# Attention memory: normalisation, query taps and the decay product put on other engines, retrieval and output products in array tiles

## The chip, the cores and the metric

The kernel runs on one core of one Trainium2 chip. The time is the device time in microseconds of one execution. The kernel before was run three times: 972.88 us is the median, 970.96 and 977.67 are the ends. The profile is that of one execution, whose span from the first to the last instruction is 973.9 us.

## The reference

The program is a block of three residual layers on x of 8 x 1024 tokens with 256 features: a mixture of experts (half weight), the attention with a memory, and the mixture of experts again. Only the attention is touched. For each batch element and chunk of 128 tokens it computes

```python
k, v, q = conv(hidden @ Wk.T), conv(hidden @ Wv.T), conv(hidden @ Wq.T)   # causal, 4 taps, per channel
alpha = (sigmoid(hidden @ aW.T + ab) * 0.1).mean(-1)                      # eta, theta alike
for c0 in range(0, S, CHUNK):
    g = grad(W_state, k[:, sl], v[:, sl]) * GRAD_SCALE                    # per token, clipped in norm
    # per token: S = eta * S - theta * g;  W = (1 - alpha) * W + S
    h = silu(einsum('btd,btod->bto', q[:, sl], W1t))
    outs.append(einsum('bto,btpo->btp', h, W2t))
out = concatenate(outs) @ Wo.T
out = out * rsqrt(mean(out * out) + EPS) * norm_g
return out * (hidden @ gW.T + gb)
```

where hidden is the layer norm of x. The kernel does not make the state of each token. It writes the retrieval as a product with the state at the chunk's start, scaled by a decay (AB), plus products of scores and gradients, weighted by scans over the tokens (M).

## The kernel before, in words

The attention takes the eight chunks (NCH = 8) of all eight batch elements at a time; most tiles are 128x1024, that is eight blocks of 128x128. Features or tokens lie on the partitions. Each engine has its own program, written out in `step(c, ...)`, and a queue runs it strictly in order; semaphores join them. `step(c)` mixes three chunks: it ends chunk c-1 (second half of its output), computes chunk c (gradients, new state, second hidden layer, retrieval, first half of the output) and prepares chunk c+1 (projections, convolution, rates, scans, gates, keys). VectorE also takes the moments of chunk c+2 (L974 to L988) and normalises it (L990). Steps 0 to 5 have this part (`norm_too`), steps 6 and 7 do not; step 7 prepares nothing.

What matters around the change:

- VectorE: after the gradients (L1141) it runs `stats_of(c+2)`, `moments_of(c+2)`, the split of the sigmoids (L1003), `convolve(c+1)` with taps on key/value and query in turn (L1012, L1019), `second_hidden(c)` (L1152, makes hid2), the last query tap (L1029), `decayed_hidden` (L1156, hid2 times AB), the momentum scans (L1034), the score product P2 (L1160), the carry and memory scans, the gate additions for pairs 0 and 1, the decay scans, `split_retrieved` (L1007), the other gate additions, and `normalise(c+2)` (L990).
- GpSimd: `gradient_norm` (power), `norm(c+2)` (power, waits for var_done), then `prep(c+1)`, and the powers and additions of the output.
- ScalarE: it copies from PSUM, makes the first query tap with the bias (L1297), the sigmoids, the copies of the new state (L1363), the second sigmoid (`second_hidden`, L1355), the rates keep and eta (L1309), the retrieved block (L1359).
- TensorE: `new_state`, `second_hidden`, `turn_state` (waits for state_copied), `rates`, `gram`, `second_scores`, `gates` 0 and 1, `retrieve`, `gates` 2 and 3 (wait for gate_read), `outputs(c, 0)`, `keys`, `hidden`, then the next step with `turn_x(c+2)` as its first part.

PSUM is cut in four pairs of banks A, BB, C, DD. `retrieve` writes 64 partitions of all of DD, one batch element after the other. `outputs` multiplies by Wo in three passes of high and low halves (`passes`, L1466), with 64 rows of the array each.

## Time and profile before

| | us |
|---|---|
| median of three runs | 972.88 |
| lowest and highest | 970.96, 977.67 |
| span of the profiled execution | 973.9 |
| TensorE busy | 794.4 (82%) |
| VectorE busy | 700.0 (72%) |
| ScalarE busy | 420.9 (43%) |
| GpSimd busy | 245.6 (25%) |

The attention takes about 255 to 766 us of the span, the first mixture of experts lies before it and the second behind it. A row of a timeline reads: start in us, duration in us, engine, line, operation, output and inputs, forms, count; at its end in brackets the time that the engine stood idle before it and what ended that. Lines are those of the kernel before.

### The profile page before, as it was taken

How to read it: one execution, taken by the hardware profiler on the slowest of the kernel's cores; microseconds unless marked ns; L12 is line 12 of the kernel's file. 1: busy time of each engine (PE TensorE's matmuls, PEld its weight loads, DVE VectorE, ACT ScalarE, POOL GpSimd, SP SyncE). 2: the span in 40 equal slices, each digit the busy share in tenths (PEclk: the TensorE clock that was granted, in tenths of full speed). 3: DMA queues.
4: the chain of work that ended last, by engine and by line, in shares of the span. 5: the costliest groups of instructions: out<-in, count | busy, mean ns of one | idle time of the engine just before them, and what ended most of it. 6: DMA issues, size and time to landing. Idle time of an engine off the chain costs nothing. (4 is left out here: it accounts for less than half of the span.)

```text
span 973.9 us, 15603 instructions
## 1 busy us (share of the span) xinstructions
PE 794.4 (82%) x5632; PEld 722.8 (74%) x5632; DVE 700.0 (72%) x1644; ACT 420.9 (43%) x837; POOL 245.6 (25%) x172
## 2 busy tenths in 40 slices
PE   5921989999266899999999999999877423999996
PEld 1311889999255788989888898989867412999996
DVE  0085759774558899999999998998832185877861
ACT  1202626542042738274573738365432103654650
POOL 0005432131101214060332414050321105423112
PEclk9955799999678999999999999999958555999999
DMA  5886842400310103012120303002020144545100
GB/s 186 301 302 181 256 162 99 152 27 15 100 43 1 44 2 115 16 60 71 44 86 0 129 0 96 33 0 86 1 87 1 50 166 146 184 128 176 54 23 28
DMA packets 58018, 88.91 MB, mean 91 GB/s; under 512 B 6705, under 2 KB 48881, under 8 KB 57841
## 3 DMA queue, kind: packets, MB, share of 16 engines
q1 hardware_dynamic: 46848, 70.44, 22.1%
q0 software_dynamic: 3840, 10.49, 3.3%
q10 hardware_dynamic: 7280, 7.34, 2.4%
q8 instruction: 28, 0.46, 0.2%
q14 instruction: 22, 0.17, 0.1%
HBM read 74.63 MB, written 22.02 MB: 99 GB/s over the span
## 5 line engine op out<-in xcount | busy, mean ns | idle before, releaser
L519 PE MATMUL ps<-weights_high_down,moe_hidden_high 128*128 128x256 f32 (+1 forms) x384 | 109.0, 284 | 2.6 <-DVE moe_rows L394 2.6
L521 PE MATMUL ps<-weights_high_down,moe_hidden_low 128*128 128x256 f32 (+1 forms) x384 | 107.9, 281 | 0.0
L520 PE MATMUL ps<-weights_low_down,moe_hidden_high 128*128 128x256 f32 (+1 forms) x384 | 107.9, 281 | 0.0
L519 PE MATMUL ps<-moe_normedT_high,weights_high_up 128*128 128x320 f32 x256 | 82.7, 323 | 2.1 <-DVE moe_hidden_low L386 1.0
L520 PE MATMUL ps<-moe_normedT_low,weights_high_up 128*128 128x320 f32 x256 | 80.7, 315 | 0.0
L521 PE MATMUL ps<-moe_normedT_high,weights_low_up 128*128 128x320 f32 x256 | 80.6, 315 | 0.0
L386 DVE SCALAR_TENSOR_TENSOR moe_hidden_low<-ps,moe_hidden_high 128x320 fp32r<-128x320 f32 x128 | 62.6, 489 | 21.1 <-ACT moe_hidden_high L481 18.3
L481 ACT ACTIVATE moe_hidden_high<-ps 128x320 fp32r<-128x320 f32 x128 | 56.2, 439 | 38.3 <-PE ps L521 25.5
L461 ACT CAST weights_high_up<-weights_raw_up 128x256 fp32r<-128x256 f32 x128 | 43.8, 404 | 64.1 <-PEq L104 64.1
L519 PEld LDWEIGHTS ps<-weights_high_down,moe_hidden_high 128*128 128x128 f32 (+1 forms) x384 | 69.3, 181 | 2.8 <-issue 2.8
L521 PEld LDWEIGHTS ps<-weights_high_down,moe_hidden_low 128*128 128x128 f32 (+1 forms) x384 | 69.4, 181 | 0.0
L520 PEld LDWEIGHTS ps<-weights_low_down,moe_hidden_high 128*128 128x128 f32 (+1 forms) x384 | 69.4, 181 | 0.0
L889 POOL TENSOR_TENSOR att_QAB<-att_Q,att_AB 128x1024 f32<-128x1024 f32 x8 | 19.0, 2376 | 195.9 <-DVE att_AB L1064 195.9
L461 ACT CAST weights_high_down<-weights_raw_down 128x256 fp32r<-128x256 f32 x128 | 45.9, 402 | 31.5 <-PE ps L521 31.5
L519 PEld LDWEIGHTS ps<-moe_normedT_high,weights_high_up 128*128 128x128 f32 x256 | 49.8, 194 | 4.7 <-issue 2.9
L1467 PE MATMUL ps<-att_w_high,att_xT_high 128*128 128x320 f32 x128 | 43.5, 340 | 11.4 <-DVE att_theta_pre L1081 11.4
L394 DVE SCALAR_TENSOR_TENSOR moe_rows<-ps,moe_prob,moe_rows 128x256 f32<-128x256 f32 (+3 forms) x48 | 23.1, 482 | 40.2 <-PE ps L521 39.5
L380 DVE TENSOR_TENSOR weights_low_down<-weights_raw_down,weights_high_down 128x256 fp32r<-128x256 f32 x128 | 49.2, 416 | 2.0 <-ACT weights_high_down L461 1.4
L520 PEld LDWEIGHTS ps<-moe_normedT_low,weights_high_up 128*128 128x128 f32 x256 | 49.7, 194 | 0.0
L521 PEld LDWEIGHTS ps<-moe_normedT_high,weights_low_up 128*128 128x128 f32 x256 | 49.6, 194 | 0.0
L380 DVE TENSOR_TENSOR weights_low_up<-weights_raw_up,weights_high_up 128x256 fp32r<-128x256 f32 x128 | 47.5, 417 | 1.5 <-ACT weights_high_up L461 1.5
L296 POOL DMA_INDIRECT moe_rows<-in_x,gather_index x20 | 24.4, 1221 | 91.9 <-issue 81.9
(240 smaller groups left out, 2346.4 us busy)
## 6 DMA issues: line engine op xcount, KB each, us to landing
weights_raw_up<-in_w SPq DMA_DIRECT2D x16, 1024.0 KB
weights_raw_down<-in_w SPq DMA_DIRECT2D x16, 1024.0 KB
xt<-in_xT SPq DMA_DIRECT2D x8, 1024.0 KB, 4.9
att_x_res<-x SPq DMA_DIRECT2D x8, 1024.0 KB, 5.5
out_x<-att_x_res SPq DMA_DIRECT2D x8, 1024.0 KB, 4.4
att_x_norm<-x ACTq DMA_DIRECT2D x7, 1024.0 KB, 5.4
att_x_norm<-x SPq DMA_DIRECT2D x1, 1024.0 KB, 5.4
att_GATE<-in_w_x SPq DMA_DIRECT2D x1, 704.0 KB
```

Of the source, the lines that this page charges most:

```text
L296: nc.gpsimd.indirect_dma_start(rows[:, j, :], None, rows_dram, bass.IndirectOffsetOnAxis(t["gather_index"][:, j:j + 1], 0), bounds_check=T ...
L380: v.tensor_tensor(weights.piece(weights.low, u, f), weights.piece(weights.raw, u, f), weights.piece(weights.high, u, f).bitcast(F32), ALU. ...
L386: v.scalar_tensor_tensor(hidden_low[i][:, f, i * D:], ps[:, 2 + (KF * i + f) % 3, 0:CAP], 0.0, hidden_high[i][:, f, i * D:].bitcast(F32), ...
L394: v.scalar_tensor_tensor(r, ps[p0:p0 + n, 6 + (NY * i + j) % 2, 0:H], prob[p0:p0 + n, tile:tile + 1], r, ALU.mult, ALU.add).then_inc(y_rea ...
L461: s.copy(weights.piece(weights.high, u, f), weights.piece(weights.raw, u, f)).then_inc(weights.high_done[u], 1)
L481: s.activation(hidden_high[i][:, f, i * D:], ps[:, 2 + (KF * i + f) % 3, 0:CAP], ACT.Relu).then_inc(relu_done, 1)
L519: mm(dst, high_l, high_r, start=start, stop=False)
L520: mm(dst, high_l, low_r, start=False, stop=False)
L521: return mm(dst, low_l, high_r, start=False, stop=stop)
L889: g.tensor_tensor(QAB[:], Q[:], AB[:], ALU.mult).then_inc(qab_ready, 1)
L1467: mm(dst, high_l, high_r, start=start, stop=False)
```

## The change

Six things change.

- `normalise(c+2)` goes from VectorE to ScalarE, as x times rstd plus shift. VectorE computes minus_mean, GpSimd multiplies it by rstd into shift. On ScalarE it stands between `new_gram(c+1)` and `retrieve(c)`; in the prologue chunk 0 is normalised first and chunk 1 ahead of the sigmoids.
- The three further query taps go from VectorE to ScalarE (product into one tile, q_part) and GpSimd (addition to Q). GpSimd also copies the halo of raw_q.
- The product of hid2 and AB goes from VectorE to GpSimd, behind the query additions.
- `retrieve` writes two batch elements to the lower and the upper 64 partitions of one bank, in turn, so the retrieved block is 128x512 instead of 64x1024; its copy and split take that form.
- `outputs` reads them from the lower and the upper 64 rows, in turn; Wo is loaded to both halves of the partitions (one more load, one wider tile).
- The key/value taps follow each other directly.

```diff
@@ -736,11 +736,11 @@
-        self.w_o = stage[0:D, cols:cols + H]
+        self.w_o = stage[:, cols:cols + H]
...
-            (self.w, d["w_x"].rearrange("(k p) n -> p k n", p=P)), (self.w_o, d["w_o"]),
+            (self.w, d["w_x"].rearrange("(k p) n -> p k n", p=P)), (self.w_o[0:D, :], d["w_o"]), (self.w_o[D:P, :], d["w_o"]),
@@ -769,13 +769,14 @@
-    w_o_high, w_o_low = sb("w_o_high", [D, H], F32R), sb("w_o_low", [D, H], F32R)
+    w_o_high, w_o_low = sb("w_o_high", [P, H], F32R), sb("w_o_low", [P, H], F32R)
...
+    minus_mean, shift = sb("minus_mean", [P, B]), sb("shift", [P, B])
@@ -788,6 +789,7 @@
+    q_part = sb("q_part", [P, B, CH])
@@ -806,7 +808,7 @@
-    retrieved_high, retrieved_low = sb("retrieved_high", [D, B, CH], F32R), sb("retrieved_low", [D, B, CH], F32R)
+    retrieved_high, retrieved_low = sb("retrieved_high", [P, HALF, CH], F32R), sb("retrieved_low", [P, HALF, CH], F32R)
@@ -818,6 +820,7 @@
+    q_taps_made, shift_ready = sem("q_taps_made"), sem("shift_ready")
@@ -853,6 +856,11 @@
     def wide(pair):
...
+    paired = DD[:, 0, :].rearrange("p (s n) -> p s n", n=CH)
...
+    def pair_of(s):
+        return [(slice(q * D, (q + 1) * D), s // 2 * HALF + 2 * q + s % 2) for q in range(2)]
...
     with nc.Block() as block:
@@ -892,6 +900,17 @@
+            def convolve_q(c):
+                for j in range(TAPS - 1):
+                    pool.wait_ge(q_taps_made, (TAPS - 1) * c + j + 1)
+                    pool.wait_ge(q_conv, TAPS * c + j + 1)
+                    g.tensor_tensor(Q[:], Q[:], q_part[:], ALU.add).then_inc(q_conv, 1)
+                g.tensor_copy(raw_q[:, :, 0:TAPS - 1], raw_q[:, :, CH:CH + TAPS - 1]).then_inc(halo_q, 1)
...
+            def decayed_hidden(c):
+                pool.wait_ge(hid2_ready, c + 1)
+                g.tensor_tensor(hid2_ab[:], hid2[:], AB[:], ALU.mult).then_inc(hid2_ab_ready, 1)
@@ -903,6 +922,8 @@
             def norm(c):
...
                 g.tensor_tensor(rstd[:], var_eps[:], t["minus_half"][:, 0:B], ALU.pow).then_inc(rstd_done, 1)
+                pool.wait_ge(rstd_done, c + 1)
+                g.tensor_tensor(shift[:], minus_mean[:], rstd[:], ALU.mult).then_inc(shift_ready, 1)
@@ -925,6 +946,9 @@
                 if not last:
+                    convolve_q(c + 1)
+                decayed_hidden(c)
+                if not last:
                     prep(c + 1, False)
@@ -935,6 +959,7 @@
             norm(1)
+            convolve_q(0)
             prep(0, True)
@@ -985,13 +1010,8 @@
                 dve.wait_ge(moments_done, B * c + B)
+                v.tensor_scalar(minus_mean[:], moments[:, :, 0], -1.0, None, ALU.mult)
                 v.tensor_scalar(var_eps[:], moments[:, :, 1], LN_EPS, None, ALU.add).then_inc(var_done, 1)
...
-            def normalise(c):
-                dve.wait_ge(rstd_done, c + 1)
-                for b in range(B):
-                    v.tensor_scalar(x_norm[:, b, :], x_norm[:, b, :], moments[:, b, 0:1], rstd[:, b:b + 1],
-                                    ALU.subtract, ALU.mult).then_inc(x_normed, 1)
@@ -1006,7 +1026,7 @@
             def split_retrieved(c):
                 dve.wait_ge(ret_copied, c + 1)
-                v.tensor_tensor(retrieved_low[:], wide(DD)[0:D, :, :], retrieved_high[:].bitcast(F32),
+                v.tensor_tensor(retrieved_low[:], paired, retrieved_high[:].bitcast(F32),
                                 ALU.subtract).then_inc(ret_split, 1)
@@ -1017,19 +1037,10 @@
             def convolve(c, par):
-                lanes = [(KV[par], raw_kv, conv_kv, kv_conv), (Q, raw_q, conv_q, q_conv)]
-                for n in range(1, TAPS - 1):
-                    for lane in lanes:
-                        tap(c, lane, n)
-                tap(c, lanes[0], TAPS - 1)
...
+                for n in range(1, TAPS):
+                    tap(c, (KV[par], raw_kv, conv_kv, kv_conv), n)
                 dve.wait_ge(kv_conv, TAPS * c + TAPS)
                 v.tensor_copy(raw_kv[:, :, 0:TAPS - 1], raw_kv[:, :, CH:CH + TAPS - 1]).then_inc(halo_kv, 1)
...
-            def convolve_rest(c):
-                tap(c, (Q, raw_q, conv_q, q_conv), TAPS - 1)
-                dve.wait_ge(q_conv, TAPS * c + TAPS)
-                v.tensor_copy(raw_q[:, :, 0:TAPS - 1], raw_q[:, :, CH:CH + TAPS - 1]).then_inc(halo_q, 1)
@@ -1153,10 +1164,6 @@
-            def decayed_hidden(c):
-                dve.wait_ge(hid2_ready, c + 1)
-                v.tensor_tensor(hid2_ab[:], hid2[:], AB[:], ALU.mult).then_inc(hid2_ab_ready, 1)
@@ -1201,9 +1208,6 @@
                 if not last:
-                    convolve_rest(c + 1)
-                decayed_hidden(c)
-                if not last:
                     momentum_scans(c + 1)
@@ -1216,8 +1220,6 @@
                     logits(c - 1)
-                if norm_too:
-                    normalise(c + 2)
                 if not last:
@@ -1233,14 +1235,11 @@
             moments_of(0)
-            normalise(0)
             split_turned(0)
...
             moments_of(1)
-            normalise(1)
             split_sigmoids(0)
             convolve(0, 0)
-            convolve_rest(0)
             momentum_scans(0)
@@ -1273,6 +1272,15 @@
+            def normalise_batches(batches):
+                for b in batches:
+                    s.activation(x_norm[:, b, :], x_norm[:, b, :], ACT.Identity, bias=shift[:, b:b + 1],
+                                 scale=rstd[:, b:b + 1]).then_inc(x_normed, 1)
...
+            def normalise(c):
+                act.wait_ge(shift_ready, c + 1)
+                normalise_batches(range(B))
@@ -1296,6 +1304,12 @@
                              scale=conv_q[:, TAPS - 1:TAPS]).then_inc(q_conv, 1)
+                q_tap(c, 0)
...
+            def q_tap(c, j):
+                act.wait_ge(q_conv, TAPS * c + j + 1 if j else TAPS * c)
+                s.activation(q_part[:], raw_q[:, :, j:j + CH], ACT.Copy,
+                             scale=conv_q[:, j:j + 1]).then_inc(q_taps_made, 1)
@@ -1358,7 +1372,7 @@
             def retrieve(c):
                 act.wait_ge(ret_made, c + 1)
-                s.copy(retrieved_high[:], wide(DD)[0:D, :, :]).then_inc(ret_copied, 1)
+                s.copy(retrieved_high[:], paired).then_inc(ret_copied, 1)
@@ -1409,12 +1423,17 @@
                     sigmoids(c + 1, False)
+                    q_tap(c + 1, 1)
                 new_state(c, par)
+                if not last:
+                    q_tap(c + 1, 2)
                 second_hidden(c)
...
                 new_gram(c + 1)
+                if load and not last:
+                    normalise(c + 2)
                 retrieve(c)
@@ -1428,11 +1447,15 @@
             new_gram(0)
+            normalise(0)
             turned(0, True)
...
             q_projection(0, True)
+            normalise(1)
             sigmoids(0, True)
+            q_tap(0, 1)
+            q_tap(0, 2)
             rates(0, True)
@@ -1576,9 +1599,11 @@
             def retrieve(c, par):
...
                 pe.wait_ge(p2_ready, c + 1)
-                for b in range(B):
-                    mm(wide(DD)[0:D, b, :], state[par][:, b, 2 * D:3 * D], hid2_ab[:, b, :], start=True, stop=False)
-                    last = mm(wide(DD)[0:D, b, :], grad_w2[:, b, :], P2[:, b, :], start=False, stop=True)
+                for s in range(HALF):
+                    for rows, b in pair_of(s):
+                        mm(paired[rows, s, :], state[par][:, b, 2 * D:3 * D], hid2_ab[:, b, :], start=True, stop=False)
+                    for rows, b in pair_of(s):
+                        last = mm(paired[rows, s, :], grad_w2[:, b, :], P2[:, b, :], start=False, stop=True)
                 last.then_inc(ret_made, 1)
@@ -1613,9 +1638,13 @@
                     pe.wait_ge(gated_ready, 2 * c + 1)
-                for b in range(HALF):
-                    last = passes(DD[:, b // 2, (b % 2) * H:(b % 2 + 1) * H], retrieved_high[:, h * HALF + b, :],
-                                  retrieved_low[:, h * HALF + b, :], w_o_high[:], w_o_low[:], True, True)
+                for s in range(2 * h, 2 * h + 2):
+                    for high, w, start, stop in ((retrieved_high, w_o_high, True, False),
+                                                 (retrieved_high, w_o_low, False, False),
+                                                 (retrieved_low, w_o_high, False, True)):
+                        for rows, b in pair_of(s):
+                            last = mm(DD[:, b % HALF // 2, (b % 2) * H:(b % 2 + 1) * H], high[rows, s, :],
+                                      w[rows, :], start=start, stop=stop)
                 last.then_inc(o_made, 1)
...
```

Line numbers in the rows of after are those of the changed kernel. On ScalarE, in the loop, from the cast of the sigmoids (att_sig_high) on: att_state and the first att_read_w are the copies of the new state, att_hid is the second sigmoid, the second att_read_w the turned copy, att_keep and att_eta the rates. Before:

```order
L1307 CAST att_sig_high<-att_mom 128x1024
L1366 COPY att_state<-ps 128x8x64
L1367 COPY att_state<-ps 128x8x128
L1368 COPY att_read_w<-ps 64x8x64
L1357 ACTIVATE att_hid<-ps 128x1024
L1372 ACTIVATE att_read_w<-ps 64x8x64
L1313 ACTIVATE att_keep<-ps 128x1024
L1315 ACTIVATE att_eta<-ps 128x1024
```

ScalarE, the same place, now:

```order
L1321 CAST att_sig_high<-att_mom 128x1024
L1310 REGISTER_ALU
L1311 ACTIVATE att_q_part<-att_raw_q,att_conv_q 128x1024
L1380 COPY att_state<-ps 128x8x64
L1381 COPY att_state<-ps 128x8x128
L1382 COPY att_read_w<-ps 64x8x64
L1310 REGISTER_ALU
L1311 ACTIVATE att_q_part<-att_raw_q,att_conv_q 128x1024
L1371 ACTIVATE att_hid<-ps 128x1024
L1386 ACTIVATE att_read_w<-ps 64x8x64
L1327 ACTIVATE att_keep<-ps 128x1024
L1329 ACTIVATE att_eta<-ps 128x1024
```

Query tap 1 now stands ahead of the state copies and query tap 2 ahead of the second sigmoid; tap 0 stands right behind the tap with the bias.

On GpSimd, in step 0, from the power of the gradient norm (att_n) to the products of prep. Before:

```order
L909 TENSOR_TENSOR att_n<-att_n,minus_half 128x8
L905 TENSOR_TENSOR att_rstd<-att_var_eps,minus_half 128x8
L889 TENSOR_TENSOR att_QAB<-att_Q,att_AB 128x1024
L890 TENSOR_TENSOR att_MIX<-att_fold,att_AB 128x8x64
L892 TENSOR_TENSOR att_MIX<-att_fold_low,att_carry 128x8x64
```

GpSimd, the same place, now:

```order
L930 TENSOR_TENSOR att_n<-att_n,minus_half 128x8
L924 TENSOR_TENSOR att_rstd<-att_var_eps,minus_half 128x8
L926 TENSOR_TENSOR att_shift<-att_minus_mean,att_rstd 128x8
L907 TENSOR_TENSOR att_Q<-att_Q,att_q_part 128x1024 x3
L908 COPY att_raw_q<-att_raw_q 128x8x3
L912 TENSOR_TENSOR att_hid_ab<-att_hid,att_AB 128x1024
L897 TENSOR_TENSOR att_QAB<-att_Q,att_AB 128x1024
L898 TENSOR_TENSOR att_MIX<-att_fold,att_AB 128x8x64
L900 TENSOR_TENSOR att_MIX<-att_fold_low,att_carry 128x8x64
```

The three additions stand behind the power of chunk c+2, and the decay product behind them.

On VectorE, in step 0, from the split of the sigmoids (att_sig_low) to the momentum scans (att_mom). Before:

```order
L1005 TENSOR_TENSOR att_sig_low<-att_mom,att_sig_high 128x1024
L1016 SCALAR_TENSOR_TENSOR att_KV<-att_raw_kv,att_conv_kv,att_KV 128x1024
L1016 SCALAR_TENSOR_TENSOR att_Q<-att_raw_q,att_conv_q,att_Q 128x1024
L1016 SCALAR_TENSOR_TENSOR att_KV<-att_raw_kv,att_conv_kv,att_KV 128x1024
L1016 SCALAR_TENSOR_TENSOR att_Q<-att_raw_q,att_conv_q,att_Q 128x1024
L1016 SCALAR_TENSOR_TENSOR att_KV<-att_raw_kv,att_conv_kv,att_KV 128x1024
L1027 COPY att_raw_kv<-att_raw_kv 128x8x3
L1154 TENSOR_TENSOR att_hid<-ps,att_hid 128x1024
L1016 SCALAR_TENSOR_TENSOR att_Q<-att_raw_q,att_conv_q,att_Q 128x1024
L1032 COPY att_raw_q<-att_raw_q 128x8x3
L1158 TENSOR_TENSOR att_hid_ab<-att_hid,att_AB 128x1024
L1037 SCALAR_TENSOR_TENSOR att_mom<-att_eta,ident 128x128 x8
```

VectorE, the same place, now:

```order
L1025 TENSOR_TENSOR att_sig_low<-att_mom,att_sig_high 128x1024
L1036 SCALAR_TENSOR_TENSOR att_KV<-att_raw_kv,att_conv_kv,att_KV 128x1024 x3
L1043 COPY att_raw_kv<-att_raw_kv 128x8x3
L1165 TENSOR_TENSOR att_hid<-ps,att_hid 128x1024
L1048 SCALAR_TENSOR_TENSOR att_mom<-att_eta,ident 128x128 x8
```

Five instructions of VectorE are gone from this place: three query taps, the halo copy and the decay product.

## Rows read from the trace of the kernel before

**Rows 1.** Stretches: start:end, length, busy PE, PEld, DVE, ACT, POOL, clock, DMA share, GB/s.

```profile
440.00:480.00 40.00, 38.32 (x313) 36.51 (x311) 38.85 (x89) 18.32 (x28) 7.16 (x5) 1.00 0.09 29
```

**Rows 2.** VectorE's timeline over one step, from gradients to gradients.

```profile
605.55 0.69 DVE L1149 TENSOR_TENSOR att_grad_w<-ps,att_n 128x512 f32<-128x512 f32 x1
...
609.57 0.17 DVE L988 TENSOR_SCALAR att_var_eps<-att_moments 128x8 f32<-128x8 f32 x1
...
612.24 1.28 DVE L1016 SCALAR_TENSOR_TENSOR att_Q<-att_raw_q,att_conv_q,att_Q 128x1024 f32<-128x1024 f32 x1
...
619.76 1.22 DVE L1158 TENSOR_TENSOR att_hid_ab<-att_hid,att_AB 128x1024 f32<-128x1024 f32 x1
620.90 2.63 DVE L1037 TENSOR_TENSOR_SCAN att_mom<-att_eta,ident 128x128 f32<-128x128 f32 x8
...
634.64 1.21 DVE L1009 TENSOR_TENSOR att_retrieved_low<-ps,att_retrieved_high 64x1024 fp32r<-64x1024 f32 x1
...
637.49 3.79 DVE L993 TENSOR_SCALAR att_x_norm<-att_x_norm,att_moments,att_rstd 128x256 f32<-128x256 f32 x8
...
652.69 1.66 DVE L1175 SCALAR_TENSOR_TENSOR att_GATE<-ps,att_o_rs,att_GATE 128x256 f32<-128x256 f32 x4 [0.23 <-POOL att_o_rs L914]
...
660.88 0.68 DVE L1149 TENSOR_TENSOR att_grad_w<-ps,att_n 128x512 f32<-128x512 f32 x1
```

**Rows 3.** TensorE's timeline: retrieval, gate products, outputs, turned keys.

```profile
626.65 0.43 PE L1580 MATMUL ps<-att_hid_ab,att_state 128*64 128x128 f32 x2
...
630.83 0.41 PE L1467 MATMUL ps<-att_w_high,att_xT_high 128*128 128x320 f32 x1 [0.47 <-DVE att_theta_pre L1081]
...
636.23 0.38 PE L1467 MATMUL ps<-att_w_o_high,att_retrieved_high 64*128 64x256 f32 x1
...
637.83 1.09 PE L1525 MATMUL ps<-ident,att_KV 128*128 128x128 f32 x8
```

**Rows 4.** Stretches around the start of the next step, columns as in rows 1.

```profile
642.00:644.00 2.00, 0.93 (x9) 0.77 (x7) 2.00 (x4) 1.54 (x2) 1.01 (x1) 0.89 0.00 0
644.00:646.00 2.00, 2.00 (x11) 2.00 (x11) 1.22 (x4) 1.15 (x3) 0.00 (x0) 0.50 0.00 0
```

**Rows 5.** GpSimd's timeline: a residual addition, the power of a norm.

```profile
599.15 2.41 POOL L921 TENSOR_TENSOR att_x_res<-att_x_res,att_GATE 128x1024 f32<-128x1024 f32 x1
...
609.82 1.64 POOL L905 TENSOR_TENSOR att_rstd<-att_var_eps,minus_half 128x8 f32<-128x8 f32 x1 [5.64 <-DVE att_var_eps L988]
```

**Rows 6.** ScalarE's timeline: cast, last state copy, second rate.

```profile
608.82 1.05 ACT L1307 CAST att_sig_high<-att_mom 128x1024 fp32r<-128x1024 f32 x1
...
613.35 0.59 ACT L1368 COPY att_read_w<-ps 64x512 f32<-64x512 f32 x1
...
618.32 1.02 ACT L1315 ACTIVATE att_eta<-ps 128x1024 f32<-128x1024 f32 x1
```

**Rows 7.** Timelines of the prologue, ScalarE and VectorE.

```profile
282.90 1.25 ACT L1297 ACTIVATE att_Q<-att_raw_q,att_conv_q 128x1024 f32<-128x1024 f32 x1
...
292.50 1.03 ACT L1315 ACTIVATE att_eta<-ps 128x1024 f32<-128x1024 f32 x1 [0.40 <-PE ps L1497]
...
296.42 2.63 DVE L1037 TENSOR_TENSOR_SCAN att_mom<-att_eta,ident 128x128 f32<-128x128 f32 x8
```

**Rows 8.** Timelines of VectorE and GpSimd where they meet.

```profile
334.38 1.22 DVE L1005 TENSOR_TENSOR att_sig_low<-att_mom,att_sig_high 128x1024 fp32r<-128x1024 f32 x1
...
334.55 2.54 POOL L905 TENSOR_TENSOR att_rstd<-att_var_eps,minus_half 128x8 f32<-128x8 f32 x1 [5.64 <-DVE att_var_eps L988]
...
701.68 2.68 POOL L921 TENSOR_TENSOR att_x_res<-att_x_res,att_GATE 128x1024 f32<-128x1024 f32 x1 [3.54 <-DVE att_GATE L1175]
```

**Rows 9.** Line 1121: count, shortest/median/longest ns, first and last start.

```profile
L1121 DVE TENSOR_TENSOR att_slope<-att_sig_h,att_slope x8: 691/692/2742, 321.3 to 702.2; 128x512 f32<-128x512 f32 x8
```

**Rows 10.** VectorE's timeline in the last chunk.

```profile
745.38 1.22 DVE L1009 TENSOR_TENSOR att_retrieved_low<-ps,att_retrieved_high 64x1024 fp32r<-64x1024 f32 x1 [5.33 <-ACT att_retrieved_high L1361]
```

## The prediction

> **What bounds the kernel now.** I read the stretch table of the attention loop first. In forty microseconds TensorE is busy 38.32 and VectorE 38.85, at full granted clock, while ScalarE and GpSimd are half idle or more [rows 1]. So two engines are full at once, and relief of VectorE alone can win only what TensorE waits for. Then VectorE's timeline gives the length of a step. I count from G, the end of the second gradient product (605.55 + 0.69 = 606.24); the next G is 661.56, so a step is 55.3 [rows 2]. There are eight chunks, six steps (chunks 0 to 5) that also normalise a chunk two ahead, one that doesn't (6), and the last. TensorE's timeline shows its few waits: 0.47 ahead of the gate products, for VectorE [rows 3], and 1.07 near 643, after which the granted clock is 0.50, the lower level of 1.2 GHz, for about three microseconds [rows 4]. Those waits and the slow stretch are some 3 us of a step, which is all that TensorE would gain from an infinitely fast VectorE.
>
> **What VectorE loses.** Per step: three query taps of 1.28 that overlap a little (3.8), the halo copy (0.1), the decay product 1.22, eight normalisations 3.79, and about half of the 1.21 split of the retrieved block, since it becomes 128x512 (0.5) [rows 2]. That is 9.4 less, and 0.1 more for the new minus_mean. This is what the change offers on paper, 9.3 of 55.3.
>
> **What the path gets instead.** The query sum now passes back and forth: GpSimd adds, ScalarE makes the next tap into the one q_part, GpSimd adds again. Both queues are in order. On GpSimd the three adds stand behind norm(c+2), which needs the moments. On ScalarE tap 1 stands ahead of the state copies, and tap 2 ahead of the second sigmoid, which releases hid2, the state's second copy, keep and eta. Prices: an add of 128x1024 is taken as the 2.41 of the residual add in the same form [rows 5]; a tap from 128x1024 of SBUF as 1.15, between the 1.05 of the cast and the 1.25 with scale and bias [rows 6, 7].
>
> The lock has to be priced too. VectorE's slope took 2.74 behind a GpSimd add that had begun at 701.68 and ended at 704.36, where elsewhere this 128x512 product takes 0.69; in the other direction GpSimd's power took 2.54 behind a VectorE split begun 0.17 earlier, where it takes 1.64 otherwise [rows 5, 8, 9]. So a VectorE instruction with two SBUF inputs and a GpSimd add do not run together, and the one that waits gets its turn when the running instruction ends. The Trainium skill (SBUF — State Buffer, Who interferes with whom) says the same: two SBUF inputs contend with a GpSimd instruction that reads SBUF. By that rule, the trace agrees, the taps and scans of VectorE count as victims, products from PSUM don't; without it the rival below would be the forecast.
>
> Now the step, in microseconds after G. The variance is ready at 3.6 (609.74 plus minus_mean), the power ends at 5.3 [rows 2, 5]. The ScalarE cast ends at 4.75, not 3.63, since tap 0 is ahead of it [rows 6]; VectorE's split of it ends at 5.95. The small shift product waits for that split; by then VectorE has begun its first key tap, so add 0 runs from about 7.2 to 9.6. Tap 1 ends at 10.75. Add 1 now meets VectorE's third tap: it starts at 10.8 or at 11.9, whoever is first; I take the first, to 13.2. Tap 2 ends at 14.4, the sigmoid (1.03) at 15.45, the turned copy at 16.0, keep at 17.0 and eta at 18.0. Before, eta ended at 619.34, which is 13.1 [rows 6]. Add 2 runs 14.5 to 16.9, the decay product on GpSimd 17.05 to 19.45, and it holds off the momentum scans, whose inputs both lie in SBUF. They start at 19.45, where they started at 14.66 [rows 2]: 4.8 late.
>
> From there the scans, score product and gate additions run as before, so the retrieved block is split at 33.1 and done at 33.8 (before 29.5). TensorE meets two new waits. Turning the state has to wait for the state copies, which ended at 7.7 and now end at 12.75 [rows 6]. The last gate products wait for gate_read until 29.2; retrieval has ended by 26.3 if its column tiles overlap. They then end at 34.5, outputs at 35.3, turned keys at 36.3, the key product at 37.5, the hidden product at 40.15. With the 3.8 of normalisation gone VectorE catches up here: hid is made at 41.4. Outputs of the second half, both splits of x, the slope and the residual keep their order; the second gated output ends at 49.5, against 48.1 before (654.35, a G later than 606.24), and the next G comes 7.3 behind it, as before (661.56 less 654.35) [rows 2]. That is a step of 56.8, 1.45 more.
>
> This sum had the turning of x at full clock. Before, the two stretches from 642 to 646 alone lose 2 x 0.50 + 2 x 0.11 = 1.2 to the clock, behind the 1.07 wait [rows 4]; I put the whole at 1.4. The new waits, 3.6 at the turned state (12.75 against some 9.1) and up to 2.9 at the gates, are longer, so I take the same 1.4 as paid behind them: nothing if it falls where TensorE has slack, 1.7 if all of it falls on the gate products. So a step is 2.85 more: 1.45 at the least with this lock, 4.4 if add 1 also loses its turn (1.1 to 1.2) and the clock costs most.
>
> **Tiles.** Retrieval takes 3.7 now (626.65 to 630.36), outputs of one half 1.6 (636.23 to 637.83) [rows 3]. No row shows two tiles at once; the bounds are nothing and half. I take half, since the pairs use different rows or columns of the array. On the path of the six steps only the two output halves count, 1.6 of gain in a step, which is in the chain above; if they don't overlap the step grows by that. The Trainium skill (TensorEngine Tiling (Array Packing), Key Properties) says different tiles run in parallel, but that changing the tiling mode drains the array. By that rule four drains a step would eat a part of it; no run here shows one.
>
> **Ends.** In the prologue ScalarE normalises chunk 0 (8 x 0.52, an estimate between a quarter and a half of the 1.25 that 1024 elements take, 0.31 and 0.62, beside VectorE's 3.79 / 8 = 0.47): 1.8 later [rows 2, 7]. Chunk 1 then stands ahead of the sigmoids, 4.2, with tap 0 at 1.15 and a wait for tap 2. Eta ended at 293.5 and scans began at 296.4, so 2.9 were spare [rows 7]; eta is now 8 later and the third add holds the scans a little: 5.5 in all, 3 if a normalisation costs 0.31. Step 6 has no norm, but its chain through the sigmoids remains: +0.5. In the last chunk the chain is bare, VectorE waits 5.33 for the retrieved block [rows 10]: retrieval 1.85, outputs 0.8 and 1.4 (half clock), copy and split 0.9 make 5; less what the logits in between fill, 4; 0.9 without overlap of tiles. The decay product's 1.2 more is hidden there by the second scores.
>
> **Sum.** 6 x 2.85 = 17.1, + 5.5 + 0.5 - 4.0 = 19.1. The sum is made on the profiled execution, whose span is 973.9, and gives 993.0. The median of the runs shown, 972.88, stands one below that span: **992.0**. About 1%, 9.7 us, is what a measurement can tell from no change.
>
> **Rivals.**
> First, the forecast chain with its own range 983 to 999 (1.45 to 4.0 a step): 0.53. For it: two in-order queues and one q_part; against: its sub-microsecond turns are estimates.
> Second, the one on the other side: GpSimd's adds don't hold VectorE off in this place. Adds then end at 7.9, 11.6 and 15.2, eta at 16.4, scans start at 16.4, 1.7 late, and the 3.8 of normalisation more than pays: a step of 54.5 to 55.3. With ends of +2 (5.5 + 0.5 - 4.0) that gives 970 to 975, **971**. It decides if the scans start less than 3 late. Against it are the two rows of the lock [rows 8, 9]; for it, those show one tensor product and one power, no scan. 0.22.
> Third, the relief is paid in full because TensorE stays dense: its 1.5 of waits, 1.5 of slow clock and 1.6 to 3.4 of tiles go, 4.6 a step, six steps 28, ends +2: **947**; half of it 961. Against: VectorE would have to be ready while ScalarE waits for two adds. 0.12.
> Fourth, tiles bring nothing (1.6 a step more, 3 at the end) or each turn is lost: 4.5 to 6 a step, **1007**. 0.13.
>
> **Numbers.** The range reaches from inside the second rival to the foot of the fourth, 966 to 1005. Slower by over 1% (above 982.6): most of the first and all of the fourth, 0.63. Within: the second and the first's foot, 0.24. Faster: 0.13.
>
> **What would show it.** VectorE's busy share falls to about 80% of the loop, with waits ahead of hid2 for the sigmoid and of the momentum scans; key taps and scans have single records longer by up to 2.4 where GpSimd adds. ScalarE waits for the adds ahead of taps 1 and 2 (about 3.5 and 0.5). TensorE waits ahead of the turned state, with a lower granted clock behind it. The momentum scans start 4 to 6 after where they did, counted from G. The forecast is wrong if scans show their old 0.4 beside GpSimd work, if taps 1 and 2 find their adds long done, or if a step is under 55.3.

## The result

The changed kernel takes 1013.98 us (median of 1011.12 to 1015.09) against 971.92 (969.65 to 977.67): ratio 1.041, 95% interval 1.037 to 1.046, 42 us slower. The forecast had 992.0, range 966 to 1005. Its direction and the first half of its mechanism were there, its size was less than half. (Of the ten runs of tiles alone, below, two fell in a slower state of the chip, and its median and ratio are those of the other eight.)

The profiled executions have spans of 1009.3 and 973.9, 35.4 apart; the medians are 42 apart. The spans are cut where both kernels do the same thing: SyncE's load of the first chunk, the end of the second gradient product of each chunk (G), and the cast of the token list in the second mixture of experts.

| stretch, us | before | after | change | forecast |
|---|---|---|---|---|
| start to the first attention load | 253.6 | 247.8 | -5.8 | 0 |
| prologue, to G of chunk 0 | 77.4 | 85.5 | +8.1 | +5.5 |
| six steps | 330.6 | 359.4 | +28.8 | +17.1 |
| step 6 | 56.1 | 56.9 | +0.8 | +0.5 |
| last chunk, to the token list | 84.7 | 85.7 | +1.0 | -4.0 |
| from there to the end | 171.6 | 174.1 | +2.5 | 0 |

The first and the last row are code that the change does not touch; the four between them add up to +38.7, where the forecast had +19.1. In the kernels below they lie at 245 to 254 and 170.6 to 174.2 with no order in them, and one indirect transfer of 4.2 us in place of 1.0 explains most of the 2.5. So spans are compared stretch by stretch, and what is under some 4 us in a whole span is left to the medians.

The page of the kernel after, its busy times, and two groups of part 5 (line, engine, output and input, count, then busy time, mean ns of one, and the idle time ahead of them):

```profile
PE 793.8 (79%) x5632; PEld 720.1 (71%) x5632; DVE 675.2 (67%) x1548; ACT 472.2 (47%) x925; POOL 343.6 (34%) x220
...
L907 POOL TENSOR_TENSOR att_Q<-att_Q,att_q_part 128x1024 f32<-128x1024 f32 x24 | 70.5, 2939 | 32.5 <-ACT att_q_part L1311 32.5
...
L1036 DVE SCALAR_TENSOR_TENSOR att_KV<-att_raw_kv,att_conv_kv,att_KV 128x1024 f32<-128x1024 f32 x24 | 50.9, 2121 | 0.6
```

An addition of 128x1024 is 2.35 when it is alone and 2.94 on the mean here; a key tap, 1.28 in [rows 2], has become 2.12. One step follows, from G at 573.10 to the next at 634.14. GpSimd's timeline (start, length, line, operation, output and input, then the idle time and who ended it):

```profile
576.76 1.64 POOL L924 TENSOR_TENSOR att_rstd<-att_var_eps,minus_half 128x8 f32<-128x8 f32 x1 [5.72 <-DVE att_var_eps L1014]
...
579.10 3.38 POOL L907 TENSOR_TENSOR att_Q<-att_Q,att_q_part 128x1024 f32<-128x1024 f32 x1
583.82 3.27 POOL L907 TENSOR_TENSOR att_Q<-att_Q,att_q_part 128x1024 f32<-128x1024 f32 x1 [1.34 <-ACT att_q_part L1311]
588.44 2.35 POOL L907 TENSOR_TENSOR att_Q<-att_Q,att_q_part 128x1024 f32<-128x1024 f32 x1 [1.35 <-ACT att_q_part L1311]
590.73 0.20 POOL L908 COPY att_raw_q<-att_raw_q 128x24 f32<-128x24 f32 x1
590.89 2.35 POOL L912 TENSOR_TENSOR att_hid_ab<-att_hid,att_AB 128x1024 f32<-128x1024 f32 x1
```

ScalarE and VectorE in the same step, beside [rows 2, 6] of before:

```profile
582.51 1.15 ACT L1311 ACTIVATE att_q_part<-att_raw_q,att_conv_q 128x1024 f32<-128x1024 f32 x1 [4.70 <-POOL att_Q L907]
...
587.13 1.16 ACT L1311 ACTIVATE att_q_part<-att_raw_q,att_conv_q 128x1024 f32<-128x1024 f32 x1 [1.61 <-POOL att_Q L907]
...
590.75 1.02 ACT L1329 ACTIVATE att_eta<-ps 128x1024 f32<-128x1024 f32 x1
```

```profile
578.99 5.89 DVE L1036 SCALAR_TENSOR_TENSOR att_KV<-att_raw_kv,att_conv_kv,att_KV 128x1024 f32<-128x1024 f32 x3
584.91 2.22 DVE L1043 COPY att_raw_kv<-att_raw_kv 128x24 f32<-128x24 f32 x1
589.23 1.23 DVE L1165 TENSOR_TENSOR att_hid<-ps,att_hid 128x1024 f32<-128x1024 f32 x1 [2.09 <-ACT att_hid L1371]
...
591.80 3.93 DVE L1048 TENSOR_TENSOR_SCAN att_mom<-att_eta,ident 128x128 f32<-128x128 f32 x8 [1.35 <-ACT att_eta L1329]
```

The turns are plain: an addition, ScalarE's next tap behind it, the next addition. Additions 0 and 1 take 3.38 and 3.27, as each first waits for a key tap that runs. The small halo copy (the last three columns of a chunk, kept for the next) takes 2.22 in place of 0.18, for it waits out addition 1. The momentum scans start at G + 18.7 and, with one of them held by the decay product, end at G + 22.6, where they ended at G + 17.3.

TensorE then stands before the last two pairs of gate products, for VectorE's gate additions. Its timeline, and stretches of 2 us (start:end, length, busy PE, PEld, DVE, ACT, POOL, then the granted clock, DMA share, GB/s):

```profile
603.03 0.42 PE L1490 MATMUL ps<-att_w_high,att_xT_high 128*128 128x320 f32 x1 [2.69 <-DVE att_theta_pre L1092]
```

```profile
602.00:604.00 2.00, 0.97 (x6) 0.97 (x7) 2.00 (x6) 0.00 (x0) 0.00 (x0) 1.00 0.00 0
604.00:606.00 2.00, 2.00 (x12) 2.00 (x10) 2.00 (x7) 0.00 (x0) 0.00 (x0) 0.57 0.00 0
606.00:608.00 2.00, 2.00 (x10) 2.00 (x10) 2.00 (x7) 0.00 (x0) 0.98 (x1) 0.50 0.00 0
608.00:610.00 2.00, 2.00 (x9) 2.00 (x8) 0.33 (x2) 0.00 (x0) 2.00 (x2) 0.50 0.00 0
610.00:612.00 2.00, 2.00 (x16) 1.98 (x17) 1.11 (x3) 0.53 (x1) 1.42 (x2) 0.72 0.00 0
```

So the clock falls to the lower level, 1.2 GHz, for some seven microseconds in which TensorE is fully busy. By whole steps, two of the kernel before and four of the kernel after (chunks 2 to 5):

```profile
440.60:495.65 55.05, 52.55 (x398) 48.34 (x396) 52.61 (x114) 31.34 (x49) 16.82 (x10) 1.00 0.18 58
...
606.24:661.56 55.32, 53.77 (x397) 49.94 (x396) 52.52 (x112) 31.24 (x49) 16.82 (x10) 0.97 0.12 38
```

```profile
453.30:511.96 58.66, 52.72 (x397) 48.32 (x396) 49.28 (x101) 37.68 (x60) 28.80 (x16) 0.94 0.17 55
511.96:573.10 61.14, 54.00 (x397) 49.33 (x396) 49.45 (x101) 37.56 (x60) 28.76 (x16) 0.92 0.16 51
573.10:634.14 61.04, 52.77 (x398) 48.51 (x397) 49.44 (x102) 37.67 (x60) 28.76 (x16) 0.94 0.15 52
634.14:692.67 58.53, 52.55 (x397) 48.27 (x396) 49.18 (x100) 37.57 (x60) 28.83 (x16) 0.94 0.11 36
```

VectorE's busy time fell by only 3.3 us a step, of the 9.3 taken off: the rest came back inside instructions that are held off. Length times one less the mean clock gives what TensorE's work loses to the clock: 0.8 us of a step before (mean of six), 4.3 after. What the step loses is less, and depends on where the clock is low. The last two rows have the same mean clock and are 2.5 apart. In the step of 61.04 it is 0.50 from G + 31 to 38, at the last gate products; in the one of 58.53 from G + 18 to 25, ahead of the retrieval, and these gate products run at 1.00. So do those of the step of 58.66. The other four steps have the lower clock at them and take 59.8 to 61.1: 1.3 us more over the mean of six (59.9 against 58.6).

### The profile page after: what moved, and what is told of

Read it like the earlier page. It is cut to its first block and busy times, and to the rows that moved or that the text cites. A ratio compares the mean times of both kernels' runs of the same rounds, so it can differ in the third digit from the quotient of the medians.

```text
span 1009.3 us, 15688 instructions
## 1 busy us (share of the span) xinstructions
PE 793.8 (79%) x5632; PEld 720.1 (71%) x5632; DVE 675.2 (67%) x1548; ACT 472.2 (47%) x925; POOL 343.6 (34%) x220
## 5 line engine op out<-in xcount | busy, mean ns | idle before, releaser
L907 POOL TENSOR_TENSOR att_Q<-att_Q,att_q_part 128x1024 f32<-128x1024 f32 x24 | 70.5, 2939 | 32.5 <-ACT att_q_part L1311 32.5
L481 ACT ACTIVATE moe_hidden_high<-ps 128x320 fp32r<-128x320 f32 x128 | 56.0, 438 | 37.5 <-PE ps L521 27.9
L1490 PE MATMUL ps<-att_w_high,att_xT_high 128*128 128x320 f32 x128 | 49.1, 383 | 19.6 <-DVE att_theta_pre L1092 19.1
L1036 DVE SCALAR_TENSOR_TENSOR att_KV<-att_raw_kv,att_conv_kv,att_KV 128x1024 f32<-128x1024 f32 x24 | 50.9, 2121 | 0.6
```

What stands on the lines that cost most here:

```text
L481: s.activation(hidden_high[i][:, f, i * D:], ps[:, 2 + (KF * i + f) % 3, 0:CAP], ACT.Relu).then_inc(relu_done, 1)
L907: g.tensor_tensor(Q[:], Q[:], q_part[:], ALU.add).then_inc(q_conv, 1)
L1036: v.scalar_tensor_tensor(y[:], x[:, :, j:j + CH], w[:, j:j + 1], y[:], ALU.mult, ALU.add).then_inc(done, 1)
L1490: mm(dst, high_l, high_r, start=start, stop=False)
```

## Experiments

"Step" is the mean of the six steps, "scans end" is where the last momentum scan ends after G. The unchanged kernel has 55.1 and 17.3, the changed one 59.9 and 22.6. Every ratio is against runs of the kernel before on the same chip.

### One part at a time

**Tiles alone:** `paired[rows, s, :]` for `wide(DD)[0:D, b, :]` in retrieval, row pairs of `w_o` in outputs, all else as before.

> The kernel before with one of the four parts: only retrieval in column tiles and output product in row tiles. Theory A (the loss of 42 us comes from the query taps: their turns between two in-order queues, the lock between GpSimd adds and VectorE, and the lower TensorE clock behind the gap that this opens at the last gate products; the other parts cost nothing or gain): tiles gain what TensorE is dense for, 1.6 us a step at the output halves and up to 1.85 at retrieval, less where VectorE (38.85 of 40 us busy) is the next limit: 0.5 to 1.6 a step and some 3 in the last chunk, 961 to 968. Theory B (every part brings a share; switching the tile shape costs TensorE time around each group): same or slower, 972 to 985. Seen in the trace: retrieval 1.85 and outputs of a half 0.8 long, without an idle stretch beside them, by theory A.

Measured: 968.4 us, ratio 0.993 (0.990 to 0.996); step 55.3, last chunk 83.1 (before 84.7). TensorE was relieved and waited instead, as its waits over 340 to 660 us show (engine and line, for whom, in all, times, longest):

```profile
PE ps L1472 <- DVE att_theta_pre L1086: 14.9, 6, 3.6
PE ps L1467 <- DVE att_P L1113: 8.2, 6, 2.3
```

Before, these two waits are 4.2 and 7.1 in all. The step gains nothing, since VectorE's end of it did not move; only the last chunk, where the chain is bare, gains 1.6. Theory A's 0.5 to 1.6 a step is refuted; the time lies at the upper edge of its range.

**Normalisation alone:** `s.activation(x_norm[:, b, :], ..., bias=shift, scale=rstd)` on ScalarE, the `tensor_scalar` of VectorE gone.

> The kernel before with only the normalisation moved from VectorE to ScalarE. Theory A: VectorE loses 3.8 us of a step, TensorE waits about 1.5 a step and loses about 1.4 to the clock, so 0 to 2.5 a step is gained in six steps, the prologue loses 3: 960 to 975. Theory B (ScalarE's eight normalisations of 0.5, which stand ahead of the copy of the retrieved block, hold that copy and with it split, outputs and keys): the copy starts later than the retrieval ends, 1 to 3 us a step lost, 980 to 992. Told apart by what ScalarE's copy of the retrieved block waits for: TensorE (A) or nothing but its own queue (B).

Measured: 975.0, ratio 1.000 (0.997 to 1.003). Step 53.8, a gain of 1.3; prologue 83.2, a loss of 5.8; last chunk 88.1, 3.4 more in a stretch where nothing is normalised, which stays unexplained. ScalarE's eight take 4.04, VectorE's took 3.79 in a step and 2.68 in the prologue. ScalarE's copy of the retrieved block still waits for TensorE (6.50 in this step), so theory B's cause falls:

```profile
454.41 4.04 ACT L1273 ACTIVATE att_x_norm<-att_x_norm,att_shift,att_rstd 128x256 f32<-128x256 f32 x8
464.95 1.01 ACT L1365 CAST att_retrieved_high<-ps 64x1024 fp32r<-64x1024 f32 x1 [6.50 <-PE ps L1589]
```

**Decay product alone:** `g.tensor_tensor(hid2_ab[:], hid2[:], AB[:], ALU.mult)` in GpSimd's step ahead of `prep`.

> The kernel before with only the decay product moved from VectorE to GpSimd. It takes 2.4 there instead of 1.2 on VectorE and stands in front of the product for QAB. Theory A: the momentum scans read only SBUF and are held off for up to 2.4, VectorE has lost 1.2, and second scores come 1.2 later at most: 0 to +1.5 a step, 972 to 983, the momentum scans' first record about 2.4 longer or their start as much later. Theory B (no lock in scans): -0.5 to 0 a step, 968 to 972, scans of 0.4 each beside the product.

Measured: 979.3, ratio 1.006 (1.003 to 1.008). Step 56.1, scans end 18.2. It is not the scans that are held off but the copy ahead of them, of 128x24 numbers:

```profile
450.71 2.23 DVE L1037 COPY att_raw_q<-att_raw_q 128x24 f32<-128x24 f32 x1
452.85 2.62 DVE L1042 TENSOR_TENSOR_SCAN att_mom<-att_eta,ident 128x128 f32<-128x128 f32 x8
```

Theory A's size is right, its victim another. The Trainium skill (SBUF — State Buffer, Who interferes with whom) counts copies on VectorE among the instructions that can shut GpSimd out and be shut out by it; by that rule, the trace agrees, 2.23 against 0.18 for the same copy of the keys, three rows earlier in that timeline.

**Query taps and tiles:** the taps as in the change, with the tiles, as the new buffer does not fit in SBUF without them.

> The kernel before with the query taps on ScalarE and GpSimd, and the tiles (without them the new buffer does not fit in SBUF); normalisation and decay product stay on VectorE. Theory A (the query taps carry the loss): at least 1005, and as VectorE keeps 5 us a step more than in the changed kernel, it could be up to 5 a step more: 1005 to 1040; a step over 60, tap 1 on ScalarE waits about 4.5 for the first add. Theory B (the parts share the loss): 985 to 1000.

Measured: 996.3, ratio 1.024 (1.020 to 1.028). Step 57.9, scans end 20.3, prologue +2.8. That is theory B's range of time: the taps carry 2.6 a step over tiles alone, most of the loss but not all. Single parts add up to 55.1 + 0.2 - 1.3 + 1.0 + 2.6 = 57.6 a step, and the change has 59.9: 2.3 a step is how they combine, 1.3 of it the clock at the last gate products.

### One part taken back

**Decay product back on VectorE**, all else changed.

> The changed kernel with the decay product back on VectorE (tiles, normalisation and query taps stay moved). The single parts of a step add up to 55.1 + 0.2 (tiles) - 1.3 (normalisation) + 2.6 (query taps) = 56.6, and with the decay product +1.0 to 57.6, where the changed kernel has 59.9. Theory A (the decay product behind add 2 is what meets the scans twice, 2.35 of GpSimd right at the place where eta is awaited, and opens the gap at the last gate products behind which the clock halves): a step of 56.5 to 57.5, some 993 to 997. Theory B (normalisation on ScalarE, 4.1 us in a queue that the taps already delay, is what does not combine): the step stays near 59 and the time near 1005.

Measured: 994.6, ratio 1.021 (1.015 to 1.027); step 57.3, scans end 21.3; the prologue is 89.2, 3.7 more than with the change, unexplained.

**Normalisation back on VectorE**, all else changed.

> The changed kernel with the normalisation back on VectorE (tiles, query taps and decay product stay moved). Single parts give 57.9 (query taps and tiles) + 1.0 (decay product) = 58.9 a step. Theory A (decay product and adds in one queue are what hurts): 59.5 to 61, since VectorE keeps 3.8 more; 1008 to 1015. Theory B (normalisation on ScalarE does not combine with the taps): 57.5 to 58.9, 995 to 1003.

Measured: 999.6, ratio 1.028 (1.022 to 1.033); step 59.4, scans end 21.4. So the decay product, 1.0 alone, is worth 2.6 a step here. Half of that, 1.3, is the scans, which end earlier without it: it stands behind the third addition, right where VectorE waits for eta. The other 1.3 is the clock: with the decay product back it is 1.00 at the last gate products in five of six steps. With the decay product back that is theory A's step and time. With the normalisation back the step lies at A's foot and the time in B's range: the prologue is 5.5 cheaper with VectorE's normalisation, which neither counted.

### Turns, length or lock

**Three buffers:** the taps go to `q_part`, `hid2_ab` and `squares`, so that ScalarE waits for no addition.

```
-                g.tensor_tensor(Q[:], Q[:], q_part[:], ALU.add)
+                g.tensor_tensor(Q[:], Q[:], q_parts[j], ALU.add)
```

> The changed kernel with the turns taken out of the query sum and nothing else: ScalarE writes the three taps into three buffers (taps 1 and 2 behind the cast of the sigmoids, ahead of the state copies; the buffers are ones that lie idle then), so no tap waits for an add. GpSimd's three adds stay and still meet VectorE's taps and scans. Theory A (the turns between two in-order queues carry the loss): state copies end 3 earlier, eta at about 14 after the second gradient product in place of 18.7, scans start 16 to 17 (the decay product still ahead or beside), a step of 56 to 57, 985 to 995. Theory B (the lock between GpSimd adds and VectorE carries it): the adds are the same work in the same place, a step of 59 to 61, 1003 to 1014.

Measured: 998.0, ratio 1.029 (1.022 to 1.036); step 58.3, scans 17.1 to 21.9. Eta now ends at G + 13.1, as in the kernel before. Without turns the additions stand back to back, and VectorE pays what ScalarE had paid:

```profile
455.42 7.98 DVE L1037 SCALAR_TENSOR_TENSOR att_KV<-att_raw_kv,att_conv_kv,att_KV 128x1024 f32<-128x1024 f32 x3
463.44 2.21 DVE L1044 COPY att_raw_kv<-att_raw_kv 128x24 f32<-128x24 f32 x1
...
466.70 4.73 DVE L1049 TENSOR_TENSOR_SCAN att_mom<-att_eta,ident 128x128 f32<-128x128 f32 x8
```

TensorE's longest wait, up to 4.2, is now for VectorE's second hidden product, queued behind these taps and the copy, and with that wait the clock falls. Neither theory holds: taking the turns away gives 1.6 of 4.8.

**Additions of one column:** `Q[:, :, 0:1]` in place of `Q[:]`, all waits kept; the other 127 columns are left out of the sum.

> The changed kernel with GpSimd's three adds cut to one column of 128 for each sequence (the other columns of the query keep the last tap and bias alone: that part of the computation is left out). All waits between GpSimd and ScalarE stay, only the adds' length and what they hold off go. Theory A (the length of the adds, 2.35 bare and 3.3 beside VectorE, and the lock with VectorE's taps carry the loss): eta at about 14 after the second gradient product, scans 15 to 18, a step of 54 to 56, 968 to 982. Theory B (the order of two queues with one buffer carries it whatever an add takes): scans from 17.5 on, a step of 57.5 or more, 990 or more.

Measured: 975.1, ratio 1.003 (0.999 to 1.006); step 54.7, scans 14.9 to 18.4. That is 5.2 a step less than the change. The order of queues and the single buffer cost next to nothing by themselves; the length of the additions, with what they hold off and what the clock adds behind them, is the whole loss of a step. Theory A's number. The prologue stays at 86.0.

**The same length without the operands:** ahead of each one-column addition a power of 128x8 numbers.

```
+                    g.tensor_tensor(power_small[:], ones_small[:], t["minus_half"][:, 0:B], ALU.pow)
```

> As the run with adds of one column (the other columns of the query again keep the last tap and bias alone), but ahead of each of the three adds GpSimd takes a power of 128x8 numbers of its own, which lasts 1.6 to 2.0 us and hardly reads SBUF: GpSimd is as long busy in each turn as with a bare add of 2.35, without an operand of 128x1024. Theory A (it is the length in the chain of turns): eta and scans come 3 x 1.8 later where the turns are in series, scans from 17 to 18, a step of 58 or more, 995 or more. Theory B (it is the lock, adds and VectorE holding each other off): key taps and scans keep their old length, adds never stretch to 3.3, a step of 55 to 57, 975 to 988.

Measured: 993.6, ratio 1.022 (1.017 to 1.027); step 58.0, scans 19.4 to 22.0, later than theory A's 17 to 18. GpSimd and VectorE:

```profile
459.04 2.67 POOL L908 TENSOR_TENSOR att_power_small<-att_ones_small,minus_half 128x8 f32<-128x8 f32 x1
461.67 1.25 POOL L909 TENSOR_TENSOR att_Q<-att_Q,att_q_part 128x8 f32<-128x8 f32 x1
464.26 1.64 POOL L908 TENSOR_TENSOR att_power_small<-att_ones_small,minus_half 128x8 f32<-128x8 f32 x1 [1.34 <-ACT att_q_part L1314]
```

```profile
458.93 3.92 DVE L1039 SCALAR_TENSOR_TENSOR att_KV<-att_raw_kv,att_conv_kv,att_KV 128x1024 f32<-128x1024 f32 x3
462.88 0.18 DVE L1046 COPY att_raw_kv<-att_raw_kv 128x24 f32<-128x24 f32 x1
```

VectorE is hardly held off any more. GpSimd itself still pays for the lock, even with eight numbers a partition: 2.67 and 1.25 in place of 1.64 and 0.22, each behind a key tap that runs.

The step is 3.3 longer than with bare one-column additions and 1.9 shorter than the change, but these two are not length and lock, for the clock has a part in both. In all six steps it is 0.50 from G + 12 to 19. The products for the rates take 0.63 there in place of 0.40 in this step, and eta comes at 19.4, later than in the change, though the second hidden product started a microsecond earlier. And in all six steps the last gate products run at 1.00, where the change has them low in four. What can be read without the clock is where VectorE's second hidden product starts after G: 12.3 with one column, 15.1 with the power, 16.1 in the change. Of these 3.9, 2.9 is length (GpSimd's own waits for the key taps included) and 1.0 the operands of 128x1024. Theory A is nearer.

### The clock

**Products that nobody reads** fill TensorE's waits: 18 gate products ahead of the wait for the state copies, 16 ahead of the last gate pairs.

```
+                for j in range(18):
+                    mm(BB[:, 0, 0:H + D], xT_high[:, 0, 0:CH], w_high[:, 0, GT_COLS], start=True, stop=True)
```

> The changed kernel with products that nobody reads put where TensorE waits in a step: 18 gate products of 128x320 (0.147 us each at full clock, 2.6 in all) ahead of the wait for the state copies, and 16 (2.35) ahead of the last two pairs of gate products. They change no wait and no order of any other engine. Theory A (the granted clock falls to its lower level after these gaps, and the 3.7 to 4.9 us of a step that are lost by it, from the mean granted clock of 0.94 to 0.92 over 60, are most of what the forecast missed behind the gates): mean granted clock in the steps 0.98 or more, a step of 57 to 58.5 in place of 59.9, 992 to 1003. Theory B (the clock has slack behind it, and the engines other than TensorE set the step): the clock rises but the step stays at 59.5 to 62, 1010 to 1025.

Measured: 1012.6, ratio 1.043 (1.037 to 1.049); step 61.6. The premise failed: the wait at the gates was gone (0.2 in all), but the clock fell all the same, now behind a gap of 1.45 that had no filler, ahead of the Gram products (`gram`, att_read_w times itself). While it is low the fillers run slower too: the last gate products end at G + 38.9 and 39.0 in two steps, where the change has 37.6 at the latest. And in two steps TensorE stood for 1.7 and 2.1 ahead of the turning of x, a gap that no engine ended by the profile.

```profile
468.00:470.00 2.00, 0.55 (x8) 0.43 (x8) 1.13 (x1) 1.95 (x3) 1.91 (x1) 1.00 0.00 0
470.00:472.00 2.00, 2.00 (x19) 1.93 (x17) 0.64 (x2) 2.00 (x4) 2.00 (x3) 0.68 0.00 0
472.00:474.00 2.00, 2.00 (x12) 2.00 (x10) 2.00 (x4) 2.00 (x5) 0.89 (x1) 0.50 0.03 8
```

**The third gap closed too**, by computing the second half of eta's mean product four times more.

> The changed kernel with the fillers of the earlier run and a third: the second half of the mean product for eta is computed four times more (1.7 us), which covers the wait ahead of the Gram products. Theory A (the clock falls behind whichever gap of TensorE is left, and its 3.7 to 4.9 us of a step are on the path): mean granted clock 0.98 or more, a step of 57 to 59. Theory B (the clock has slack, or falls without a gap): a step of 60 or more.

Measured: 1005.3, ratio 1.035 (1.029 to 1.040) where the change has 1.041; step 59.05, scans still end at 22.7. Three steps by stretches:

```profile
390.67:449.33 58.66, 56.38 (x439) 51.65 (x438) 49.31 (x102) 37.62 (x60) 28.80 (x16) 1.00 0.17 55
449.33:508.58 59.25, 56.19 (x439) 51.88 (x439) 49.28 (x102) 37.40 (x60) 28.88 (x16) 1.00 0.18 55
508.58:567.43 58.85, 56.40 (x439) 51.69 (x439) 49.31 (x102) 37.81 (x60) 28.99 (x16) 1.00 0.17 54
```

Five of six steps are at full clock; in the sixth it is low from G + 43 to 47. The step is 0.85 shorter, where the arithmetic of the mean clock had 4.0 to offer (4.3 less the 0.3 left). Two of the six steps again have a gap of TensorE that no engine ended, here of chunk 2:

```profile
492.36 1.94 PE L1485 MATMUL ps<-ident,att_x_norm 128*128 128x128 f32 x16 [1.82 <-issue]
```

The four without it take 58.6 on the mean, the same as the two steps of the change whose last gate products run at 1.00. So the clock was worth 1.3 a step, all of it at the last gate products, and the rest of the low stretches lay beside waits of other engines.

**Where ScalarE prepares theta:** its absolute value, table load and exponential stand behind the hidden sigmoid.

```
+                    hidden(c + 1, False)
+                    thetas(c + 1, False)
```

> The changed kernel with ScalarE's absolute value and exponential of theta (0.63, a table load of 1.28, 0.63) put behind the sigmoid of the hidden product in place of ahead of the squares. Nothing waits for them before the next step's logarithm. Theory A (ScalarE's serial run of 6.5 us from the last gate addition sets when hid is made): hid up to 0.8 to 2.0 earlier, until it waits for the hidden product on TensorE; a step 0.8 to 1.5 less, 58.4 to 59.1, 1003 to 1009. Theory B (TensorE's products at the lower clock set it): no change, 59.9 a step, 1012 to 1016.

Measured: 1012.6, ratio 1.041 (1.036 to 1.045); step 60.6. The question was what sets the start of hid, 6.6 after the last gate addition (7.6 before, with the normalisations in between). ScalarE's run got 2.5 shorter, and hid started 6.2 after it, for the sigmoid now waits for TensorE, which does outputs, turned keys, key product and hidden product in the same time:

```profile
495.98 0.60 ACT L1353 ACTIVATE att_sig_h<-ps 128x512 f32<-128x512 f32 x1 [1.91 <-PE ps L1563]
```

And the moved functions now stand ahead of the casts of x, for which VectorE waits 1.11, and of the copy of the turned keys, for which TensorE waits 1.9 in every step (0.8 at most in the change). So 0.4 was won at hid and more than that lost behind it. That two chains of nearly equal length end at hid is shown; that theory A's time fails for this reason alone is not, since the move also delayed the keys.

### Versions that beat the kernel before

**Tiles and normalisation:** query taps and decay product back on VectorE.

> Tiles and the normalisation on ScalarE, query taps and decay product on VectorE as before. Alone the normalisation won 1.3 us a step and tiles nothing, by theory because VectorE (38.85 of 40 us busy) was the limit with tiles alone and TensorE with the normalisation alone. Theory A (two engines full at once, so relief pays only if both get it): more than the sum, 2 to 3.5 us a step, 953 to 962. Theory B (the clock or a chain through both sets the step): the sum, 1.3 a step, 962 to 970.

Measured: 969.0, ratio 0.995 (0.992 to 0.998); step 54.1, prologue 82.7: theory B's time, the reliefs do not multiply. In the two steps at full clock it is 53.3, 0.5 under normalisation alone; three others, with the lower clock behind the wait at the gates, take 54.4 to 55.7. **Prologue's two chunks normalised on VectorE again:**

> A version to beat the kernel before: tiles, and normalisation on ScalarE for the chunks that are normalised inside a step (two ahead), while the prologue's two chunks are normalised on VectorE as before; query taps and decay product stay on VectorE. The run with tiles and all normalisations on ScalarE had 54.1 a step against 55.1, but 82.7 in the prologue against 77.4. Theory A (both sizes add): 5 us less than that run's 969, 962 to 965, prologue 77.5 to 78.5. Theory B (prologue time was a matter of a disturbed transfer): no difference, 969.

Measured: 965.0, ratio 0.993 (0.991 to 0.996); prologue 78.4, step 54.4, last chunk 85.8. **And fillers in the last chunk**, 18, 28 and 4 products in TensorE's waits:

> The same with products that nobody reads in the last chunk: 18 of 128x320 ahead of the first turning of the result, 28 ahead of the state product, 4 ahead of the retrieval, where TensorE waits and its granted clock is 0.50 to 0.73 afterwards (the state product of the last chunk takes 10.3 us there). Theory A (the last chunk's chain runs through TensorE at the lower level): state and second hidden product 4 to 6 us shorter, 956 to 960. Theory B (the filler delays what it precedes as much as the clock gives): 962 to 966.

Measured: 960.4, ratio 0.989 (0.984 to 0.993); last chunk 77.6, 8.2 less in the profiled execution, while the medians are 4.6 apart. **And 14 ahead of the last gate pairs of each step:**

> The fastest version so far (tiles, normalisation on ScalarE inside the steps, fillers in the last chunk; 54.1 a step, 960.4) with 14 more gate products that nobody reads (2.1 us) ahead of the last two pairs in each step, where TensorE waits 2.4 on average, up to 3.7, the only gap of over 1 us in its step. Theory A (clock on the path): granted clock from 0.97 to 0.99 or more, a step of 52.5 to 53.5, 951 to 957. Theory B (VectorE sets the step there and the clock has slack): 54 to 55, 960 to 966.

Measured: 955.5, ratio 0.983 (0.979 to 0.987), the fastest, 17 us below the kernel before. Step 53.35 in place of 54.06, clock 0.99 in place of 0.97: theory A, with 0.7 a step. **With theta's functions last as well:**

> The fastest version so far (53.35 a step, 955.5) with theta's absolute value and exponential put behind the sigmoid in the same way. Theory A: 0.8 to 1.3 a step less, 946 to 951. Theory B: no change, 954 to 957.

Measured: 957.3, ratio 0.983 (0.979 to 0.986), step 54.3, 1.0 more: nothing gained, as in the changed kernel. TensorE again waits 1.9 for the copy of the turned keys in every step.

## Why the prediction was wrong

**The chain of turns and the lock: right.** Forecast and measured, after G: tap 1 ends at 10.75, was 10.6; add 1 ran 10.8 to 13.2, was 10.7 to 14.0; tap 2 ended 14.4, was 15.2; eta 18.0, was 18.7; scans start 19.45, was 18.7; state copies 12.75, was 12.4; TensorE's wait for them 3.6, was 3.1. Scans ended at 22.6, by the forecast's steps at 22.1. The additions' price of 2.41 was right and the second turn was lost in part, 0.9, which the forecast had put aside as its worse case. Additions of one column show that the cause is the one named; how its length and the lock share it is only sized up to the second hidden product (2.9 and 1.0).

**Behind the scans: the step that failed.** From scans' end to the next G the forecast had 56.8 - 22.1 = 34.7 at full clock, where the kernel before has 37.8. That is 3.1 of relief, and it says "With the 3.8 of normalisation gone VectorE catches up here". The runs, step less scans' end:

| kernel | scans end | step | difference |
|---|---|---|---|
| before | 17.3 | 55.1 | 37.8 |
| decay product alone | 18.2 | 56.1 | 37.9 |
| query taps and tiles | 20.2 | 57.9 | 37.7 |
| normalisation back | 21.4 | 59.4 | 38.0 |
| normalisation alone | 17.3 | 53.8 | 36.5 |
| adds of one column | 18.4 | 54.7 | 36.3 |
| power in the adds' place | 22.0 | 58.0 | 36.0 |
| decay product back | 21.3 | 57.3 | 36.0 |
| all gaps filled, four steps without the gap of 1.8 | 22.6 | 58.6 | 36.0 |
| fastest version | 17.3 | 53.35 | 36.05 |
| changed kernel, two steps with full clock at the gates | 22.6 | 58.6 | 36.0 |
| changed kernel, mean | 22.6 | 59.9 | 37.3 |

With the normalisation on ScalarE, the tiles, and full clock at the last gate products it is 36.0 in kernel after kernel, whatever stands ahead of the scans. So 1.8 of the 3.1 came: 1.3 by the normalisation, 0.5 by the tiles. The other 1.3 a step, 8 us of the 11.7 missed in six steps, is the step that failed.

With the decay product back, a kernel at full clock at the gates in five of six steps, the pieces are, measured and forecast: scans' end to the end of the outputs 13.7 and 13.2, to hid made 6.9 and 6.1, to the second gated output 8.2 and 8.1, to G 7.2 and 7.3. The largest miss is the 0.8 at hid, the place where VectorE was to catch up. There hid starts 6.5 after the last gate addition, where it was 7.6, for two other chains end there (ScalarE's two table loads and squares, TensorE's keys and hidden product). Those chains were not laid out in the forecast, which followed VectorE past them. Of the rest, 0.2 is a slip: by its own rows TensorE resumes at the gates 7.3 after the scans, and it took 7.1. (It also has the key product at 37.5, where its rows give 38.3; nothing hangs on that.)

**The clock: right in size.** Forecast 1.4 a step, and worth 1.3, at the last gate products, as it said (four of six steps); the 4.3 of the mean clock are not what it costs. The scans end 0.5 later than forecast. So 1.3 + 0.5 - 0.1 make 1.7 a step against 59.9 - 58.15 = 1.75 missed. The table of stretches shows 1.95, since the forecast took one step of 55.3 as its base and the mean is 55.1.

**Ends.** Prologue +8.1, forecast 5.5: normalisation alone costs 5.8, query taps 2.8. The two stretches of 4.0 on ScalarE were priced right (1.8 net and 4.2); the 2.9 counted as spare between eta and the scans [rows 7] was not slack: VectorE's taps follow the cast and its split, and these moved by 5.9 as well (normalisation alone; 6.1 in the change). Last chunk +1.0, forecast -4.0. Tiles gain 1.6 there (alone), not 4. The chunk's clock has a large part in the rest: in the kernel before it is 1.00 from the scores to the retrieval, in the changed one 0.50. Stretches of 4 us, from 24 after that chunk's G, before and after:

```profile
741.60:745.60 4.00, 4.00 (x38) 3.83 (x36) 0.22 (x1) 1.01 (x1) 0.00 (x0) 1.00 0.00 0
```

```profile
773.50:777.50 4.00, 4.00 (x35) 3.65 (x35) 0.00 (x0) 0.06 (x1) 0.00 (x0) 0.50 0.00 0
```

The fillers in the last chunk show that this is on the path: they took 8.2 out. Last chunks came out at 83.0 to 83.2 in seven kernels and at 85.7 to 85.8 in six, the changed one among them, and the clock sorts them. In all seven it is back near 1.00 from G + 27 to 30, in all six it stays at 0.50 from G + 21 on. What makes it stay high in one kernel and fall in another stays open.

**The rivals.** That the additions hold nothing off (971) falls by 5.89 for three key taps. Relief paid in full (947) falls by tiles alone and normalisation alone: 0 and 1.3 a step. The fourth, 4.5 to 6 a step, has the size that came (4.8), but by luck: turns were lost only in part, and "tiles bring nothing" was half right, and in the wrong way. Both groups run in half the time (retrieval 598.38 to 600.34, a half of the outputs 0.9), and the step feels 0.5 of it at most. The range was too narrow because its upper end took the lost turn and the clock, the first rival's 4.4 a step at most, and had no case in which the relieved engine's place is taken at once by the next.

## What to carry to other kernels

Before crediting a relief, lay out every chain that ends where the relieved engine is next waited for; here two engines were full, the next chains stood 1 to 2 us behind, and that gap was all that the relief was worth (1.8 of the 3.1 counted on). Work moved to GpSimd as additions with operands in SBUF costs there, costs VectorE's two-input instructions and even its tiny copies, and costs again when another queue waits for it: here 5.8 us a step (59.9 against 54.1 with both moves undone; 58.6 against 53.3 in steps with full clock at the gates) to take 5.1 off VectorE. A few products that nobody reads, in TensorE's waits, were worth 9.5 us (965.0 to 955.5). And a mean clock does not price anything by itself: two steps with the same 0.94 were 2.5 apart, by where the low stretch lay.

## What the runs showed of the hardware

- A VectorE copy of 128x24 numbers from SBUF to SBUF took 2.2 us beside GpSimd's product or addition, 0.18 otherwise (decay product alone, three buffers, and the changed kernel). The other way, GpSimd's addition of 128x8 numbers took 1.25 beside a key tap, 0.22 alone, and its power 2.67 beside a key tap, 1.64 alone (the run with a power).
- Eight scans of 128x128 with both inputs in SBUF took 3.93 and 4.73 beside GpSimd's product, 2.63 alone. One scan waits until GpSimd's instruction ends (1.72 in the changed kernel), the others run as ever (0.39).
- The granted clock fell to 0.50 some 1.2 us after TensorE had resumed at 603.03, and held for about 7 us of full work; with two gaps filled it fell behind the third, with all three filled it stayed at 1.00 in five of six steps.
- Pairs of column tiles and of row tiles took half the time of the untiled products (retrieval 2.0 for 3.7, outputs of a half 0.9 for 1.6), and the retrieval began as the logits ended, at 598.38, with no idle time of TensorE at the change of shape. The Trainium skill (TensorEngine Tiling (Array Packing), Key Properties) says that a change of tiling mode drains the array; if it does so here, it takes less than these rows can show.
